# The softmax maxima of eight heads in one round in place of four, in a planned transformer stack on one core

## The reference

```python
s = jnp.einsum('bqhd,bkhd->bhqk', q, k) * scale
a = jax.nn.softmax(s, axis=-1)
o = jnp.einsum('bhqk,bkhd->bqhd', a, v)
```

## Time and profile before

| | |
|---|---|
| median of three runs | 998.14 us (991.89 to 1003.66) |
| the profiled execution's own time | 996.28 us |
| its span, first to last instruction | 994.5 us |
| PE busy | 919.2 us |
| DVE busy | 707.8 us |
| ACT busy | 557.4 us |
| POOL busy | 146.9 us |
| mean granted TensorE clock | 0.973 of full |

### The profile page before, as it was taken

How to read it: one execution, slowest core, us unless ns; L and a number is a source line. 1 busy time by engine, 2 the same in 40 slices (tenths; PEclk the granted TensorE clock), 3 DMA queues, 4 the chain that set the end, 5 groups by cost and what they waited for, 6 DMA issues and landing times.

```text
span 994.5 us, 15383 instructions
## 1 busy us (share of the span) xinstructions
PE 919.2 (92%) x4986; PEld 398.0 (40%) x4986; DVE 707.8 (71%) x1933; ACT 557.4 (56%) x1035; POOL 146.9 (15%) x388
## 2 busy tenths in 40 slices
PE   3848999999899999999999988998999999999998
PEld 3622433444334334454445443343333433324344
DVE  5578899889788737543455568686997998886542
ACT  5023555555555567783545463366666566675773
POOL 2012120200101102110111110012112011022210
PEclk9777999999999999999999997999999999999999
DMA  8050332211112020200202060016024013121201
GB/s 305 16 143 2 84 113 67 65 37 37 49 40 75 2 65 7 63 7 1 64 8 64 7 181 12 6 39 155 7 65 130 9 34 81 38 81 41 66 2 43
DMA packets 65811, 57.49 MB, mean 58 GB/s; under 512 B 18895, under 2 KB 62915, under 8 KB 65476
## 3 DMA queue, kind: packets, MB, share of 16 engines
q1 hardware_dynamic: 64484, 54.73, 19.9%
q10 hardware_dynamic: 1248, 1.77, 0.5%
HBM read 31.01 MB, written 24.49 MB: 56 GB/s over the span
## 4 chain that ended last, share of the span: by engine, by line
PE 79%; DVE 10%; issue 4%; ACT 4%; DMA 1%; POOL 1%; SPq 0%; ACTq 0%; DVEq 0%; POOLq 0%
PE pv_bank L1540 15%; PE bank L1495 11%; PE bank L1518 10%; PE bank L1520 5%; PE bank L1522 4%; PE bank L1498 3%; PE bank L1651 3%; PE bank L1599 3%; PE bank L1600 2%; PE bank L1646 2%; DVE bank L1271 2%; PE bank L1633 2%; PE bank L1506 2%; PE bank L1565 2%; PE bank L1468 2%
## 5 line engine op out<-in xcount | busy, mean ns | idle before, releaser
L1019 ACT ACTIVATE pr<-bank 128x512 f32<-128x512 f32 (+1 forms) x704 | 379.3, 597 | 221.9 <-PE bank L1520 107.3
L1495 PE MATMUL bank<-ks,qs 97*128 97x512 bf16 x512 | 179.5, 396 | 19.3 <-issue 15.0
L1274 DVE TENSOR_REDUCE mx<-bank 128x1 f32<-128x512 f32 x256 | 162.7, 682 | 36.1 <-PE bank L1495 35.3
L1271 DVE CUSTOM_DVE_ANT_0 bank<-bank,mask_q 128x512 f32<-128x512 f32 x256 | 170.8, 710 | 23.6 <-PE bank L1495 22.3
L1518 PE MATMUL bank<-qs,ks 103*128 103x512 bf16 x512 | 181.4, 388 | 3.2 <-DMA qs<-mrow 2.4
L1540 PE MATMUL pv_bank<-pr,va 128*32 128x512 f32 x1024 | 138.0, 611 | 0.0
L1276 DVE TENSOR_REDUCE mx<-bank 128x4 f32<-128x308 f32 x192 | 83.7, 470 | 40.4 <-PE bank L1498 39.0
L1495 PEld LDWEIGHTS bank<-ks,qs 97*128 97x128 bf16 x512 | 45.7, 100 | 135.7 <-issue 31.0
L1520 PE MATMUL bank<-mask_k,identb 128*128 128x512 bf16 x256 | 98.2, 383 | 0.0
L915 POOL CAST mp<-mx 128x16 bf16<-128x16 f32 x80 | 16.1, 201 | 554.0 <-DVE mx L1271 197.4
L1518 PEld LDWEIGHTS bank<-qs,ks 103*128 103x128 bf16 x512 | 49.5, 99 | 72.9 <-issue 8.9
(11 more groups left out here) (219 smaller groups left out, 1194.2 us busy)
## 6 DMA issues: line engine op xcount, KB each, us to landing
qs<-q_parts SPq DMA_DIRECT2D x40, 384.0 KB, 4.6
q_parts<-xn SPq DMA_DIRECT2D x20, 384.0 KB, 2.6
ks<-k_parts SPq DMA_DIRECT2D x32, 192.0 KB, 4.5
q_parts<-xn SPq DMA_DIRECT2D x20, 256.0 KB, 2.3
k_parts<-u SPq DMA_DIRECT2D x8, 384.0 KB, 2.4
q_parts<-u SPq DMA_DIRECT2D x20, 128.0 KB, 2.3
qs<-mrow SPq DMA_DIRECT2D x160, 6.0 KB
late<-late_w SPq DMA_DIRECT2D x1, 2432.0 KB, 13.2
```

The source lines that it names most:

```text
L1019: act.activation(pr[0:K, 4 * (group % NSLOT) + t % 4, :], bank(k)[0:K, :], ACT.Exp, scale=SCALE).then_inc(act_done, 1)
L1271: dve.tensor_tensor_reduce(b[:, :], b[:, :], mask_q[:, qb, :], 1.0, -3e38, ALU.add, ALU.max, dst[:, qb, g, e:e + 1]).then_inc(dve_done, 1)
L1274: dve.tensor_reduce(dst[:, qb, g, e:e + 1], b[:, :], AX.X, ALU.max).then_inc(dve_done, 1)
L1495: ins = pe.matmul(b[:, :], qs[s][0:R, g, qb * P:(qb + 1) * P], ks[s][0:R, e, g, :], start=True, stop=True)
```

## The change

A round of `max_parts`, `max_t` and `max_rows` now serves two head groups (a *half*, eight heads) in place of one. The buffers `mx`, `mp` and `mr` are laid out for this, the four transposes turn 24 rows at once, the copy to `mrow` takes 24 partitions, and four DMAs carry the rows of the half, on one semaphore. There are two rounds in an attention in place of four, 40 in all in place of 80. The number of DMAs is as before (160), each with the same 6 rows. The exponentials' wait is now at the first tile of each half, and so is DVE's wait before it writes over `mx`. The DVE's wait for rows landed earlier (in `max_t`) is now for the same half of the attention before. `cmaskf` and `cbias` (used by DVE alone) are now one buffer each, shared between lanes. The planner's assumed durations of the two changed steps grow, and its other numbers (`EAGER`, `URGE`, `TABLE_KEPT`, `FAIR`, `CAP`) are all different, so that nearly every step's place moves.

```diff
-TABLE_LOAD, TABLE_KEPT = 1.3, -110.013
+TABLE_LOAD, TABLE_KEPT = 1.3, -150.9585
...
         if kind == "exp":
             a, hg, t = rest
-            first, second = [me("sp", "max_rows", a, hg), ("dve", (1, "e2_out", 2)), ("dve", (1, "mask_t", TB - 1))], []
+            first, second = [me("sp", "max_rows", a, hg // 2), ("dve", (1, "e2_out", 2)), ("dve", (1, "mask_t", TB - 1))], []
...
         if kind == "max_parts":
-            return [me("dve", "max", *rest, tiles(rest[0]) - 1)], []
+            return [me("dve", "max", rest[0], 2 * rest[1] + 1, tiles(rest[0]) - 1)], []
...
-        mx = per("mx", [P, 2, TB, 2, 2]); mr = per("mr", [P, TB * 2, 2]); mp = per("mp", [P, 2, TB, 2, 3, 2], BF16)
-        mrow = per("mrow", [44, T], BF16)
+        mx = per("mx", [P, 2, TB, 2, 2, 2]); mr = per("mr", [P, TB * 4, 2]); mp = per("mp", [P, 2, TB, 2, 2, 3, 2], BF16)
+        mrow = per("mrow", [56, T], BF16)
...
-                def max_rows(k, s, a, hg):
-                    sp.wait_ge(dve_done, count("dve", (s, "max_t", a, hg)))
-                    for g in range(2):
-                        sp.dma_start(qs[s][MROW:ROWS, 2 * hg + g, :], mrow[s][32 * (hg % 2) + 6 * g:32 * (hg % 2) + 6 * g + 6, :]).then_inc(mrows[s][hg], 16)
+                def max_rows(k, s, a, half):
+                    sp.wait_ge(dve_done, count("dve", (s, "max_t", a, half)))
+                    for g in range(4):
+                        sp.dma_start(qs[s][MROW:ROWS, 4 * half + g, :], mrow[s][32 * half + 6 * g:32 * half + 6 * g + 6, :]).then_inc(mrows[s][half], 16)
...
-                def max_t(k, s, a, hg):
+                def max_t(k, s, a, half):
                     dve.wait_ge(pe_done, count("pe", k))
-                    if hg >= 2:
-                        dve.wait_ge(mrows[s][hg - 2], 32 * (a + 1))
-                    elif a:
-                        dve.wait_ge(mrows[s][hg + 2], 32 * a)
-                    dve.tensor_copy(mrow[s][32 * (hg % 2):32 * (hg % 2) + 12, :], bank(k)[:, :].bitcast(BF16)[32 * (hg % 2):32 * (hg % 2) + 12, 0:T]).then_inc(dve_done, 1)
+                    if a:
+                        dve.wait_ge(mrows[s][half], 64 * a)
+                    dve.tensor_copy(mrow[s][32 * half:32 * half + 24, :], bank(k)[:, :].bitcast(BF16)[32 * half:32 * half + 24, 0:T]).then_inc(dve_done, 1)
...
-                def max_t(k, s, a, hg):
-                    pe.wait_ge(pool_done, count("pool", (s, "max_parts", a, hg)))
+                def max_t(k, s, a, half):
+                    pe.wait_ge(pool_done, count("pool", (s, "max_parts", a, half)))
                     b = free_bank(pe, k)[:, :].bitcast(BF16)
                     for t in range(TB):
-                        ins = pe.transpose(b[32 * (hg % 2):32 * (hg % 2) + 12, t * P:(t + 1) * P], mp[s][:, hg % 2, t].rearrange("p g c e -> p (g c e)"), identb[:, :])
+                        ins = pe.transpose(b[32 * half:32 * half + 24, t * P:(t + 1) * P], mp[s][:, half, t].rearrange("p i g c e -> p (i g c e)"), identb[:, :])
                     ins.then_inc(pe_done, 1)
...
-                    if t == 0:
-                        pe.wait_ge(mrows[s][hg], 32 * (a + 1))
+                    if t == 0 and hg % 2 == 0:
+                        pe.wait_ge(mrows[s][hg // 2], 64 * (a + 1))
```

More of the change, by code:

```diff
@@ L212 @@
          "ctx_norm": (2.5,), "rope": (.86, .82), "part1": (.56,), "parts": (1.85,), "v": (.89, .6), "ctx_t": (.25, .7),
-         "ctx_k": (.8, .8), "gate_cols": (.3,), "ctx_v": (.88, 1.9), "gates": (.4, .5), "ctx_split": (1.62,), "max_parts": (1.1,),
+         "ctx_k": (.8, .8), "gate_cols": (.3,), "ctx_v": (.88, 1.9), "gates": (.4, .5), "ctx_split": (1.62,), "max_parts": (1.25,),
          "max_t": (.32, .33), "pv": (1.03,), "pv_out": (.5,), "heads_t": (.44, .8), "attn_t": (.44, .5), "attn_out": (.89, .65),
@@ L226 @@
 BANKS, MAX_BANKS, EXP_BANKS, PV_BANKS = 6, 2, 3, 2
-TABLE_LOAD, TABLE_KEPT = 1.3, -110.013
+TABLE_LOAD, TABLE_KEPT = 1.3, -150.9585
 RUN_OF = {("mlp_h", 0): True, ("mlp_h", FC - 1): False, ("gate_h", None): True, ("expert_h", 2 * E - 1): False}
-EAGER = {"chain": 0.4061, "rows": 0.4045, "max": 0.1342, "exp": 0.0302, "pv": -0.0958, "tables": 0.3117}
-URGE = ((0.233, 0.023, -0.615, -0.375, 0.275, 0.059, -0.328, -1.935),
[3 rows of a table removed]
+EAGER = {"chain": 0.405787, "rows": 0.20422, "max": 0.156793, "exp": -0.013918, "pv": -0.057384, "tables": 0.50076}
+URGE = ((0.60302, 0.19241, -0.53655, -0.32547, 0.22721, 0.07726, -0.62221, -1.85527),
[3 rows of a table added]
 CLOSING, CORE_PHASE = ("attn_out", "mlp_add", "l1_add"), {0: 0, 1: 1, 2: 4, 3: 5, 4: 6}
-FAIR, CAP = 0.00245, 33.3072
+FAIR, CAP = 0.0027022, 49.29134
 class Order:
@@ L269, in before @@
                 first.append(("dve", self.maxima[-MAX_BANKS]))
-            if t == 0 and len(self.rows[lane]) >= 2:
+            if t == 0 and hg % 2 == 0 and len(self.rows[lane]) >= 2:
                 second.append(("pool", self.rows[lane][-2]))
@@ L294, in before @@
         if kind == "max_parts":
-            return [me("dve", "max", *rest, tiles(rest[0]) - 1)], []
+            return [me("dve", "max", rest[0], 2 * rest[1] + 1, tiles(rest[0]) - 1)], []
         if kind == "max_t":
-            a, hg = rest
-            landed = [("sp", row) for row in ([(s, "max_rows", a, hg - 2)] if hg >= 2 else [])]
-            return [me("pool", "max_parts", *rest)], landed
+            return [me("pool", "max_parts", *rest)], []
         if kind == "max_rows":
@@ L454, in open_lane @@
                     streams[lane]["max"] += [(s, "max", a, hg, t) for hg in range(HG) for t in range(tiles(a))]
-                    streams[lane]["rows"] += [(s, kind, a, hg) for hg in range(HG) for kind in ("max_parts", "max_t", "max_rows")]
+                    streams[lane]["rows"] += [(s, kind, a, half) for half in range(HG // 2) for kind in ("max_parts", "max_t", "max_rows")]
                     streams[lane]["exp"] += [(s, "exp", a, hg, t) for hg in range(HG) for t in range(tiles(a))]
@@ L619, in build @@
         cvar = per("cvar", [NK, 2]); crstd = per("crstd", [NK, 2])
[L620 to L621 removed]
+        cmask = per("cmask", [P, NK], U8); cmaskf = shared("cmaskf", [P, NK]); cany = per("cany", [P, 1])
+        cbias = shared("cbias", [P, NK], BF16)
         g_o0 = per("g_o0", [P, D]); g_co = per("g_co", [P, D])
@@ L707, in build @@
         qread = [[sem(f"q_stacked{s}_{h}") for h in range(2)] for s in range(B)]; kread = [[sem(f"k_stacked{s}_{h}") for h in range(2)] for s in range(B)]
-        mrows = [[sem(f"max_rows{s}_{hg}") for hg in range(HG)] for s in range(B)]
+        mrows = [[sem(f"max_rows{s}_{half}") for half in range(2)] for s in range(B)]
         stored = [sem(f"stored{s}") for s in range(B)]
@@ L905, in ln_rstd, with max_parts @@
                     pool.tensor_tensor(rstd[s][:, :], var[s][:, :], eps_pow[:, 0:1].to_broadcast([P, TB]), ALU.pow).then_inc(pool_done, 1)
-                def max_parts(k, s, a, hg):
-                    pool.wait_ge(dve_done, count("dve", (s, "max", a, hg, tiles(a) - 1)))
+                def max_parts(k, s, a, half):
+                    pool.wait_ge(dve_done, count("dve", (s, "max", a, 2 * half + 1, tiles(a) - 1)))
                     at = PARTS[s % LANES].index(k)
@@ L912, in max_parts @@
                         pool.wait_ge(pe_done, count("pe", max_t_of(PARTS[s % LANES][at - 2])))
-                    m = mx[s][:, hg % 2].rearrange("p t g e -> p (t g) e")
-                    part = mp[s][:, hg % 2].rearrange("p t g c e -> p (t g) c e")
+                    m = mx[s][:, half].rearrange("p t i g e -> p (t i g) e")
+                    part = mp[s][:, half].rearrange("p t i g c e -> p (t i g) c e")
                     link(pool, pool_link, n, pool.tensor_copy(part[:, :, 0, :], m))
```

8 lines of the change are left out of this document (3 added, 5 removed), and 6 rows, old and new, of the table URGE.

## The result

The changed kernel takes 1035.35 us (median, 1033.82 to 1037.14), the kernel before beside it 1000.57: ratio 1.036 [1.029, 1.043]. It is 3.6% slower. The forecast was 994.6, with a range of 979 to 1009. The profiled execution has a span of 1035.4 us, 40.9 more than before.

A forecast was written before the change was run, and what follows sets the result against it. The prediction took PE, busy for 92% of the span, to bound the kernel. From 996.28 us it summed -16.8 (rounds), +15.1 (start), -4 (layer 3) and +4 (rows' latency) to 994.6 us, range 979 to 1009.

The forecast's parts named there:

- In the middle PE is never free: Middle of the kernel before: PE busy 49.96 of 50 us, so PE work taken away there comes back as time.
- idle time of PE in the middle: Sign of a wrong forecast: PE idle mid-kernel because DVE's work is packed more densely in layer 3; no size given.
- Rows' latency: Each round's rows land later, as four DMAs on one queue add two issues (1.4 us): +4 us, between 0 and 21.
- rival B: Rows' latency decides, PE standing in its order until the fourth DMA lands: 1012 or 1029 us; chance 0.12.
- waits of PE for `qs<-mrow` of 4 us: Sign of a right forecast: PE waits for the rows in some ten places, 4 us in all.
- What a round costs PE: Maxima's turns: a round takes 0.42 us of PE whatever the rows' width, so 40 rounds fewer give -16.8 us.
- The start: First attention: keys' stack 12.5 us later, more tiles +8.8, PE work done ahead -6.2; together +15.1 us.
- Rival A: The start costs little, 5 us in place of 15: 984.5 us, or 977; chance 0.25.
- Layer 3's first self attention: Fewer tiles stand alone there (2.7 us) and stack waits are better covered (1.3): -4 us, between 0 and -8.
- the wait for the stacks ahead is better covered: Layer 3's first self attention: an estimated 1.3 us won, part of its -4 us.
- the bound of 6 us from issue to maximum: Program's start, kernel before: from SP's issue of the keys' stack (59.41) to PE's first maximum (65.65), 6.2 us.

The follow-up runs named there:

- e3: Changed kernel's order replayed, planner told that the keys' stack waits for the buffer holder's last exponential, later steps filling in: 1020.33 us.
- e9: e3 with the split, plus 14 matmuls of no use ahead of the first maximum of layer 3's attention in all four lanes: 1003.15 us.
- e4: Changed kernel, same order, with 14 matmuls of no use ahead of six first maxima (four handovers, two of layer 3's): 1022.23 us.
- the split: Each four heads' exponentials wait only for their own two of a round's four row DMAs: 1009.81 us in e3, 1028.43 us in the changed kernel.
- e8: Kernel before, with each group of four turns of the maxima done twice: 1013.91 us (1.015).
- e10: e7 with the program's first exponentials made, in the planner, to wait for the rows of eight heads: 999.28 us (1.003).
- e5: e3 with lane 1's context written out and read back behind the keys' stack on the SP queue, at least 267 steps moved: 1022.60 us.
- e7: Kernel before (rounds of four heads, own tables) with e3's edit of the planner: 994.05 us (0.995).
- e11: e7 with 8, 11 and 5 matmuls of no use ahead of layer 3's first maxima in lanes 0, 1 and 2: 996.33 us (0.997).

## Why the prediction was wrong

**The step that failed** is in the first part: "In the middle PE is never free", read from one window of before, and taken over to an order in which nearly every step had moved. I wrote that the forecast would be wrong by "idle time of PE in the middle", and gave DVE as its cause; there was no term for it. What the runs showed in its place is PE waiting for keys. The larger part is the keys' handover, in the order that I had at hand: a PE row that needs `ks` straight behind the exponentials that free it, while SP's issue and the landing (3.6 us or more) stand between. Covered at four places, it gave 15 of the 34.8 us between the kernels' medians (`e3`). The half-clock work behind layer 3's first maxima is 6.7 more (`e9`); there the buffer was free, and the keys come late by their own way through the queue, as lane 1's rows show. The clock's 10 to 13 us of `e4` are behind four handovers and two of layer 3's waits, so they lie partly in the 15 and partly in the 6.7 and are not to be added.

**Rows' latency, +4 between 0 and 21.** The mechanism was right (rival B in small) and the size off: 7 in the kernel's own order, 10.5 in the filled one, for the two issues that the split takes away. I had counted shortages and let most of them go, "since PE is slowed by DVE in the same stretches". They didn't go. The sign that I gave, waits of PE for `qs<-mrow` of 4 us, came true (4.4 in four places), but it couldn't show this size.

**What a round costs PE, -16.8.** The width of the turn didn't matter, as said. The turns' group in the changed kernel (busy us, mean ns of one, idle before); before, the mean was 222 ns:

```profile
L1502 PE MATMUL bank<-identb,mp 128*24 128x128 bf16 x160 | 16.3, 227 | 6.0 <-POOL mp L916 5.5
```

The sum's -16.8 is 40 rounds at 0.42. `e8` shows that PE's time in turns is on the path, at 0.22 a group (8.8 us for 40). Whether the 0.20 more, for the group's start and the matmul ahead, came back too, no run tells.

**The start, +15.1.** The steps came in the forecast's order, a little later. Forecast were the keys' stack near 72, the first maximum at 78.1 and the first exponential at 106.8; measured are 76.5, 80.6 and 108.6. The changed kernel's SP queue and PE timeline:

```profile
76.47 1.86 SPq L863 DMA_DIRECT2D ks<-k_parts  x4
```

```profile
80.57 20.27 PE L1491 MATMUL bank<-ks,qs 97*128 97x512 bf16 x35 [2.68 <-issue]
103.39 0.60 PE L1502 MATMUL bank<-identb,mp 128*24 128x128 bf16 x4 [2.55 <-POOL mp L916]
...
108.59 0.58 PE L1514 MATMUL bank<-qs,ks 103*128 103x512 bf16 x1 [1.50 <-DVE mx L1269]
```

35 tiles in 20.27 us are 0.58 each, near the 0.65 priced. What a first exponential so late is worth at the end stays uncertain: 14.4 us of it cost 5 to 8 in rounds of four (`e10`), and 3.6 us of it gave nothing back in rounds of eight (`e5`, with the order changed elsewhere too). The first lane's last exponential of its first half came at 137.4 (117.3 before), and that of its attention at 171.8 (157.2), so 15 us late. Rival A, "the start costs little", holds in part for rounds of four. Its lower price, 977, doesn't come out of its terms: 984.5 less 4 and less 2 is 978.5.

**Layer 3's first self attention, -4.** It isn't there. In its 50 us from the first maximum on, PE has 45.27 us of work at clock 0.85, and had 45.17 at 0.83. Busy time and clock by window, changed kernel first, then before:

```profile
628.00:678.00 50.00, 45.27 (x137) 17.73 (x138) 37.57 (x73) 13.99 (x20) 1.94 (x5) 0.85 0.12 30
```

```profile
590.00:640.00 50.00, 45.17 (x163) 19.14 (x164) 38.80 (x79) 15.00 (x31) 3.52 (x13) 0.83 0.13 35
```

PE stands there 2.60 us for the keys, 2.01 for POOL and 2.15 for the rows, where it stood 2.11, 2.52 and 0.41 before: some bare tiles were filled, and a wait for the four DMAs came in their place. The 1.3 us for "the wait for the stacks ahead is better covered" went the other way: the waits for keys at layer 3's four first maxima are 12.6 us in all, and were 6.9.

**The ledger.** From 1035.35: handovers -15.0, rows -10.5, layer 3's clock -6.7 make 1003.15, against 998.8 before. The same telling gave the kernel before 4.7 us as well (`e7`), so against that kernel the gap left is 9 us and not 4. What is left, +4 to +9 us, holds the start less the turns' gain, with a part that has no run of its own: at the forecast's +15.1 - 16.8 it would be -1.7, at +15.1 - 8.8 it is +6.3. The second fits better; that is arithmetic and not shown, and it leaves out the standing at layer 3's four waits (5.7 us more than before), which no run took away.

**The rivals.** B ended on the right side and for a part of the reason ("PE stands in its order"), but it named the rows, a third of what was found, and had a chance of 0.12. The wait for keys deserved to be a rival of its own: the shown SP queue had the keys' stack, and the bound of 6 us from issue to maximum was used at the start only.

## What to carry to other kernels

When a static order changes, go through each buffer that lanes share, and look in the new order at what stands between the last reader and the first user: if that is less than the issue and landing of the refill (3.6 us or more here), an engine will stand there, whatever its idle time was before. A planner that isn't told of a wait which the code has will place work right behind it; put the same condition in both. Where the buffer is free and the user waits all the same, look at what stands ahead of the transfer in its queue. When several transfers are bundled into one round, let each consumer wait for its own part of them, since the issues of one queue come one after another.

## What the runs showed of the hardware

- A wait can cost more than its length. Behind PE's waits of 3.65 and 3.97 us about 6 us ran at half clock; behind one of 2.72 us nothing did. The length alone doesn't decide it: behind layer 3's waits of 2.60, 3.41, 3.38 and 3.18 us and the handover of 3.71, between 3.3 and 5.5 us ran at half clock, and behind before's wait of 2.61 us (682.12) nothing did. The changed kernel at 141.70 and at 332.48 us:

```profile
141.70 0.59 PE L1491 MATMUL bank<-ks,qs 97*128 97x512 bf16 x2 [2.72 <-issue]
142.13 0.38 PE L1514 MATMUL bank<-qs,ks 103*128 103x512 bf16 x1
...
332.48 1.01 PE L1491 MATMUL bank<-ks,qs 97*128 97x512 bf16 x2 [3.65 <-issue]
333.28 1.06 PE L1449 MATMUL bank<-early,xn 128*128 128x128 f32 x4
334.27 1.94 PE L1536 MATMUL pv_bank<-pr,va 128*32 128x512 f32 x8
```

- Work of no use was worth its place there: 84 matmuls of no use made the kernel 13 us faster (`e4`). At waits of 1.1 to 2.8 us, 24 of them gave nothing (`e11`).
- The start isn't the same in each execution: the first keys' stack was issued at 76.5 us in one and 73.4 in another of the same order up to there.
